# Moving neighbour-row exchange to SyncE transfers and layer-norm scaling to ScalarE in an early-fusion kernel

## The reference, cut to what matters

```
# images: x (8, 1, 256, 256), ten steps of a filter
u = sigmoid(o / 0.5); q = 0
for _ in range(10):
    q = max(q - 0.5 * ((u[y+1] - u[y]) * vf1 + (u[x+1] - u[x]) * vf0), 0)
    Tq = (vf1*q)[y] - (vf1*q)[y-1] + (vf0*q)[x] - (vf0*q)[x-1]
    u = sigmoid((o - Tq) / 0.5)
h_img = (o - Tq) / 0.5                                   # (8, 256, 256)
# text: (8, 128) tokens, width 256, 4 layers, 16 heads, hidden 1024
h = emb[tokens] + positions
for layer in 4: h = norm(h + attention(h) @ Wc) * g1 + e1
                h = norm(h + relu(h @ W1 + b1) @ W2 + b2) * g2 + e2
# fusion: 256 image rows and 128 text rows of each sample
h = concatenate([h_img, h_txt], axis=1)                  # (8, 384, 256)
h = h + window_attention(norm(h)) @ Wo.T + bo            # 8 heads, 2 kv heads, window 64, a sink
y = square(relu(norm(h) @ W_fc.T)) @ W_proj.T
h = h + count_of_spikes(y) / 5                           # five levels of y
```

## Time and profile before

| | |
|---|---|
| median of 3 runs | 1062.35 us (1060.9 to 1063.59) |
| the profiled execution's own time | 1059.45 us |
| its span, first to last instruction | 1057.5 us |
| PE busy | 945.2 us, 89% |
| DVE busy | 900.7 us, 85% |
| ACT busy | 636.8 us, 60% |
| POOL busy | 87.9 us, 8% |
| transfers | 28.67 MB, mean 27 GB/s |
| mean granted TensorE clock | 0.982 of full |

### The profile page before, as it was taken

One profiled execution on the slowest core, in us unless ns is written; L12 is line 12 of the kernel. 1 busy time (PEld: TensorE's weight loads), 2 busy tenths in 40 slices (PEclk: granted clock), 3 DMA queues, 4 the chain that ended last, 5 costly groups with the idle time before them and its releaser, 6 DMA issues.

```text
span 1057.5 us, 18395 instructions
## 1 busy us (share of the span) xinstructions
PE 945.2 (89%) x6972; PEld 714.7 (68%) x6992; DVE 900.7 (85%) x1318; ACT 636.8 (60%) x2105; POOL 87.9 (8%) x149
## 2 busy tenths in 40 slices
PE   3589999889889989989989988789998999999997
PEld 2367777667667767767767766566666766667675
DVE  4999999999999999999999999798699699543542
ACT  1666667766666666666766665446455564745633
POOL 6100010001010010010010001010000001000000
PEclk9799999999999999999999999999999999999999
DMA  7600000110000110000110000000000000100000
GB/s 162 244 1 2 1 30 6 46 61 1 1 31 11 43 39 21 1 31 11 46 55 2 1 21 2 1 11 2 26 1 26 9 18 1 46 25 2 16 1 30
DMA packets 13544, 28.67 MB, mean 27 GB/s; under 512 B 2704, under 2 KB 9232, under 8 KB 12176
## 3 DMA queue, kind: packets, MB, share of 16 engines
q1 hardware_dynamic: 13072, 26.44, 7.5%
q0 software_dynamic: 384, 1.05, 0.6%
HBM read 22.25 MB, written 5.24 MB: 26 GB/s over the span
## 4 chain that ended last, share of the span: by engine, by line
PE 45%; DVE 43%; ACT 7%; issue 4%; DMA 1%; SPq 0%; POOL 0%; POOLq 0%; ACTq 0%; DVEq 0%
PE ps_t L595 8%; PE ps_t L604 7%; PE ps_s L493 4%; DVE neg_max L1544 4%; PE ps_m L808 3%; PE ps_t L797 3%; DVE f L1538 2%; DVE f L1520 2%; DVE f L1516 2%; DVE f L1519 2%; DVE p L1526 2%; DVE f L1511 2%; DVE p L1523 2%; DVE f L1508 2%; DVE f L1533 2%
## 5 line engine op out<-in xcount | busy, mean ns | idle before, releaser
L1010 ACT ACTIVATE prob<-ps_s,neg_max 128x128 f32<-128x128 f32 x512 | 180.1, 379 | 52.2 <-DVE neg_max L1544 52.2
L595 PE MATMUL ps_t<-hT_f,w 128*128 128x256 f32 x512 | 133.0, 404 | 33.1 <-ACT hT_f L1022 17.2
L595 PEld LDWEIGHTS ps_t<-hT_f,w 128*128 128x128 f32 x512 | 95.3, 196 | 58.9 <-ACT hidT L1076 23.9
L1018 ACT ACTIVATE probT<-ps_t 128x512 f32<-128x512 f32 x128 | 77.2, 603 | 83.2 <-PE ps_t L554 52.6
L604 PE MATMUL ps_t<-w,hidT 128*128 128x256 f32 x512 | 125.4, 383 | 0.0
L1010 ACT ACTIVATION_READ_ACCUMULATOR prob<-ps_s,neg_max 128x1 f32 x512 | 112.8, 220 | 0.0
L604 PEld LDWEIGHTS ps_t<-w,hidT 128*128 128x128 f32 x512 | 91.1, 190 | 12.2 <-issue 3.0
L797 PE MATMUL ps_t<-km,w_fc 128*128 128x384 f32 x256 | 94.4, 504 | 1.7 <-ACT km L1183 1.0
L554 PE MATMUL ps_t<-ident,prob 128*128 128x128 f32 x512 | 81.4, 283 | 5.9 <-ACT prob L1010 3.7
L1076 ACT ACTIVATE hidT<-ps_t,b 128x256 f32<-128x256 f32 x128 | 54.8, 491 | 49.8 <-PE ps_t L595 49.8
L554 PEld LDWEIGHTS ps_t<-ident,prob 128*128 128x128 f32 x512 | 63.0, 145 | 28.4 <-issue 11.8
(11 more groups left out here) (172 smaller groups left out, 1879.3 us busy)
## 6 DMA issues: line engine op xcount, KB each, us to landing
w<-in_w SPq DMA_DIRECT2D x8, 1024.0 KB, 4.9
w_attn<-in_w_attn SPq DMA_DIRECT2D x4, 768.0 KB, 4.6
out<-w SPq DMA_DIRECT2D x7, 384.0 KB, 2.4
o_all<-in_o SPq DMA_DIRECT2D x4, 512.0 KB, 10.5
filtered<-f_out SPq DMA_DIRECT2D x4, 512.0 KB, 2.6
x<-filtered SPq DMA_DIRECT2D x8, 256.0 KB, 2.7
vf<-in_vf SPq DMA_DIRECT2D x4, 256.0 KB
w_attn<-in_w_attn SPq DMA_DIRECT2D x4, 256.0 KB, 3.1
```

The costliest lines, as they stand in the source:

```text
L595: last = mm(ps_t[:, 0, D * (m % 2):D * (m % 2) + D], w1[:, c, P * m:P * m + P], hT_f[:, c], start=(c == 0), stop=(c == KC - 1))
L1010: last = A(prob[:, n % 2, hh], ps_s[n % 2][:, hh], ACT.Exp, scale=-1.0, bias=neg_max[:, n % 2, hh:hh + 1], accum_out=den)
L1018: A(probT[:, 4 * half:4 * half + 4].rearrange("p h k -> p (h k)"), ps_t[:, 1], ACT.Copy).then_inc(s["act_pT"], 1)
```

## The change

1. **Neighbour rows.** `u` and `p1` get a fifth row. SP copies it from the neighbouring partition inside SBUF, two transfers of 63 partitions by 1 KB for each of `rows_below` and `rows_above`. The 80 products on PE go, and so do the bank `halo`, the small DVE instructions 1515 and 1537, and the 128x768 forms. Now the whole difference down and the whole divergence down are one pass of 128x1024 each, and wait for a transfer.
2. **The freed bank** (`ps_y`, `row_bank`) takes the attention residual, the turned rows and the odd parts of `ff1`; the even parts stay in `ps_t`, so that `ff1(f, j)` waits for `hidden_out(f, j - 2)`.
3. **Norms on ACT.** POOL also makes `shift = -mean * rstd` (four instructions for two) and ACT scales rows as `rstd * x + shift`. This holds for all norms but the second norm of the last layer and the first `norm_x`. ACT also copies text rows and values; the bias of the values goes into `values_in`.
4. **Orders.** Lists of all engines are written anew, the loads of images and fusion weights are spread over blocks 0 to 5, and on SP the copies are placed between the other transfers.

```
@@ PE
-            def rows_below(it):
-                pe_.wait_ge(s["act_tanh"], it + 1)
-                mm(halo[:, 0], up_shift[:], u[:, 0, 0:IMG], start=True, stop=True).then_inc(s["pe_halo"], 1)
@@ SP
+            def rows_below(it):
+                if it < ITERS * PAIRS:
+                    sp.wait_ge(s["act_tanh"], it + 1)
+                    for at in (0, 64):
+                        sp.dma_start(u[at:at + 63, RPP, 0:IMG], u[at + 1:at + 64, 0, 0:IMG]).then_inc(s["halo_u"], 16)
+            def rows_above(it):
+                sp.wait_ge(s["dve_flux"], it + 1)
+                for at in (0, 64):
+                    sp.dma_start(p1[at + 1:at + 64, 0], p1[at:at + 63, RPP]).then_inc(s["halo_p"], 16)
@@ DVE
...
-                link(stt(fa[:, RPP - 1], halo[:, 0], edge[:], u[:, RPP - 1, 0:IMG], ALU.add, ALU.subtract))
+            def differences_down(it):
+                dve.wait_ge(s["halo_u"], 32 * it + 32)
+                link(tt(fa, u[:, 1:, 0:IMG], u[:, 0:RPP, 0:IMG], ALU.subtract))
                 link(tt(fa, fa, vf[:, 0], ALU.mult))
...
             def divergence(it):
-                dve.wait_ge(s["pe_halo"], 2 * it + 2)
-                link(tt(fa[:, 0], p1[:, 0], halo[:, 1], ALU.subtract))
+                dve.wait_ge(s["dve_flux"], it + 1)
+                dve.wait_ge(s["halo_p"], 32 * it + 32)
+                link(tt(fa, p1[:, 1:], p1[:, 0:RPP], ALU.subtract))
@@ ACT
+            def norm_attn(k):
+                act.wait_ge(s["pool_shift_a"], k + 1)
+                scaled_rows(k, row_bank, rstd_a, shift_a).then_inc(s["act_ln1"], 1)
+            def norm_ffn(k):
+                act.wait_ge(s["pool_shift_f"], k + 1)
+                scaled_rows(k, ps_t[:, 0], rstd, shift).then_inc(s["h_ready"], 1)
@@ PE, ff1
-                else:
-                    pe_.wait_ge(s["act_ff1"], 4 * k + j)
+                elif j >= 2:
+                    pe_.wait_ge(s["act_ff1"], 4 * k + j - 1)
...
             def block_step(a, f, it, its):                        # on ACT
                 exps(a, 0, 0)
-                exps(a, 0, 1)
+                values_out(a)
+                norm_attn(f)
                 probs_out(a, 0, 0)
                 ffn_in(f)
+                exps(a, 0, 1)
...
+                rden_out(a, 0)
                 rden_out(a, 1)
-                filter_out(it + 1)
+                if its > 1:
+                    filter_out(it + 1)
                 if a + 1 < BLOCKS:
-                    keys_out(a + 1, 0)
                     queries_out(a + 1)
                 else:
                     queries_biased(0)
+                if f < BLOCKS - PAIRS:
+                    norm_ffn(f)
```

More of the change, by code:

```diff
@@ L336, in _ @@
             for n in range(B):
+                it = TEXT_ITERS + sum(FUSE_ITERS[:n])
+                for i in range(FUSE_ITERS[n]):
+                    rows_above(it + i)
+                    rows_below(it + i + 1)
+                    pair_done(it + i)
                 if n + 2 < B:
-                    if n + 2 == B - 2:
-                        store_pair(PAIRS - 1)
-                        sp.wait_ge(s["st_img"], 16 * PAIRS + 16)
+                    sp.wait_ge(s["st_img"], 16 * ((n + 2) // 2) + 32)
                     sp.wait_ge(s["f_y"], n + 1)
@@ L963, in fuse_last @@
                 ff_in(f, 2)
+                ff_out(f, 0, range(0, 1))
                 ff_in(f, 3)
@@ L990, in first_tanh @@
             def first_tanh(pair):
-                A(u[:, :, 0:IMG], o_all[:, pair], ACT.Tanh).then_inc(s["act_tanh"], 1)
+                A(u[:, 0:RPP, 0:IMG], o_all[:, pair], ACT.Tanh).then_inc(s["act_tanh"], 1)
             def filter_out(it):
@@ new lines, in fuse_step, with fuse_late @@
+                z_out(n - 1)
+                queries_biased(n + 1)
+                values_in(n + 1)
+                keys_biased(n + 1)
+                norm_y(n)
+                z_last(n - 1)
+                if its > 1:
+                    filter_out(it + 1)
+                window_values(n + 1)
+            def fuse_late(n):
+                x2_out(n - 1)
+                if n + 1 < B:
+                    copy_text(n + 1)
+                relu_out(n - 1, 0)
+                square(n - 1, 0)
+                relu_out(n - 1, 1)
+                square(n - 1, 1)
+                tile_exps(n, 0, 0)
+                relu_out(n - 1, 2)
+                tile_exps(n, 0, 1)
@@ L1582, in scaled_rows, with norm_ffn_last @@
+                moments(rows_of(ps_t[:, 0]), 2, s["dve_stat_f"])
+            def norm_ffn_last(k):
+                dve.wait_ge(s["dve_stat_f"], k + 1)
+                dve.wait_ge(s["pool_rstd_f"], k + 1)
+                hp, rows = h[:, 2 * (k % PAIRS):2 * (k % PAIRS) + 2], rows_of(ps_t[:, 0])
+                scaled = [tick(stt(hp[:, t], rows[:, t], mv[:, t, 0:1], rows_last[:, 0], ALU.subtract, ALU.mult)) for t in range(2)]
                 for t in range(2):
                     dve.wait_ge(s["chain"], scaled[t])
-                    last = stt(hp[:, t], hp[:, t], rstd_[:, t:t + 1], rows_last[:, 1], ALU.mult, ALU.add)
@@ L1851, in fuse_late @@
                 moments_y(n)
-                norm_y(n)
                 count_spikes(n - 1, 0)
```

778 lines of the change are left out of this document (400 added, 378 removed).

## The result

The changed kernel takes **1108.2 us** (median of 4 runs, 1107.1 to 1109.7) against 1061.6 before (4 runs, 1060.8 to 1063.6): ratio 1.0437, 95% interval 1.0416 to 1.0458. The forecast was 1030.5 us, range 1014 to 1052. It was wrong in sign.

The account below looks back on a forecast made before the run. DVE was taken to bound text, PE close behind, and PE to bound fusion. 1059.45 - 21.0 - 4.2 (text) + 3.7 (start) - 10.2 (fusion) = 1027.7 us profiled, 1030.5 as median; range 1014 to 1052.

Parts of the forecast that it names:

- Part 1: DVE work in a steady text block: falls from 39.15 to 36.83 us without small forms, both norms and a wait.
- Part 2: Next text block's first DVE pass, no longer covered by norm_ffn, waits 0.57 us for Tanh; block 37.40 us, 1.75 less.
- Part 3: Copies of neighbour rows in text blocks: a pair lands after 2.4 us, inside 3.4 us of other DVE work, costing nothing.
- Part 4: PE in a text block: work 34.1 us fits in 37.4, row chain 0.5 us slower, DVE stays bound by 0.8.
- PE and ACT hold the block: Rival for text blocks: they stay near 38.5 to 39 us, gaining 0.4 instead of 1.75; 1050 us, chance 0.15.
- Part 5: Start: differences_down(0) waits for a copy queued behind 2.5 MB, there at about 30 us; +3.7 us (0 to +5.5).
- Part 6: Fusion, bound by PE: halo products -5.4, PE's waits -3.6, fuse_first about 2 us gained, last norm_y +0.8; sum -10.2 us.
- the pair serializes: Rival for the copies: two full landings one after the other, 3.9 us, each wait up to 0.5; 1051 us, chance 0.07.

Follow-up runs that it names:

- e6: The changed kernel with one wait added: DVE stands behind the first norm's moments until POOL's shift_a is there, in text blocks and the first fusion step; 1074.1 us, ratio 1.0112.
- e12: e10 with DVE's second head maximum right behind the moments and the wait for POOL behind that maximum; 1056.2 us, ratio 0.9934 to the kernel before.
- e1: The changed kernel with head_max(a, 1) moved on DVE's list from behind flux_rows to right behind moments_attn; 1088.8 us, ratio 1.0252 to the kernel before.
- e3: The changed kernel with eight unread products of 128x256 on PE between turn_probs(a, 0, 0) and turn_ffn(f); 1078.0 us (one run).
- e8: e7 with eight unread PE products before the turn of the rows and the first pair of copies issued ahead of two 1 MB loads; 1061.0 us, ratio 0.9983.
- e7: e6 with the same DVE wait for POOL behind the moments of the y rows in fusion too; 1067.9 us, ratio 1.0058 to the kernel before.
- e10: e8 with ACT's fusion list reordered: norm_x(n + 1) behind o_out(n), z_last(n - 1) ahead of norm_y(n); 1058.9 us, ratio 0.9974 to the kernel before.

## Why the prediction was wrong, by its own steps

- **Part 1, right.** 36.83 us of DVE work in a block: 36.83 and the waits shown make 40.88 of 40.91, and in e6 38.79 of 38.77.
- **Part 2, right** in mechanism: 0.46 us of wait for Tanh instead of 0.57.
- **Part 3, right that copies cost nothing in a block, mis-sized by a microsecond.** I had a pair there 2.4 us (2.1 to 3.1) after the producer. In e12 `flux_rows` starts at 302.88 and lasts 1.22, and the pass on copied rows starts at 307.71, **3.6 us** after its end. The cover of 3.4 to 3.5 us is about as long, so in the changed kernel hardly a wait shows (3.6 us in 6 places); where e1 and e12 took the maximum out of that cover it showed at once. Issuing a pair takes 1.44 us on SP, 0.72 each, where I had taken 0.43; the other 0.9 us lies in the landing.
- **Part 4, the step that failed.** "Moments, then four POOL instructions instead of two, then ACT instead of DVE, about 0.5 us more." I priced POOL's instructions by rows in which DVE read PSUM beside them, and the change itself put other passes there. The chain took 3.6 us, not 1.4, and PE's wait before the turn 3.60 us. The second half, "PE idles some 2.7 us around `turn_ffn` and `ff1(f, 0)`", costed PE's idle time but not the slower products after it: 2.2 us a block (e3). The row chain, from moments to turn, got 4.81 - 2.21 = 2.6 us longer and not 0.5. PE's work itself was right: 34.03 us in a block of e6 at a granted clock of 1.00, forecast 34.1. "DVE stays the bound with 0.8 us to spare" was then off by 4.4. The rival "PE and ACT hold the block" named the right place, and its sign was seen (DVE waits for PE before the maxima, 54.9 us in 16 places), but it had the wrong mechanism and half the price; it ended at 1050.
- **Part 5, mis-sized**: +7.1 instead of +3.7, outside its bound of 5.5. The first pass on copied rows starts at 33.19 us, after a wait of 7.9, not at 30.3. The small copies queued behind 2.5 MB came last. Issued ahead of the two 1 MB loads (e8) they cost 1.6 us over before.
- **Part 6, wrong in sign**: +17.6 instead of -11.0. The halo products went, but three costs came, by the profiles' stages: the clock on entering from the text stage (5.7 us between e7 and e8, e7's being a slow execution), the y chain held by passes (4.2, e6 to e7), the x chain seen through ACT's order (3.9, e8 to e10). The sum of 13.8 leaves 3.8 us over before, which no run here explains; ACT's longer lists remain the candidate. The forecast gain of 11.0 had no term for any of them.
- **The rival "the pair serializes"**, at 1051: not in the form it had, two full landings one behind the other. In e12 the pair of `p1` is issued from 304.13 on, and two stretches hold its data (last column GB/s), before DVE goes on at 307.71:

```profile
305.35:306.05 0.70, 0.70 (x5) 0.62 (x4) 0.70 (x1) 0.70 (x3) 0.00 (x0) 1.00 0.30 92
306.05:306.85 0.80, 0.80 (x6) 0.70 (x5) 0.45 (x1) 0.80 (x6) 0.00 (x0) 1.00 0.30 86
```

  The second copy's data moves 0.7 us behind the first's, which is the distance of the two issues. Whether copies issued closer together would queue, no run here shows.

The profile of the kernel before held the warning: in its fusion stage the `pow`, on 128x3 there, took 0.85 us in most steps and 1.73 and 1.92 in others (at 689.29 and 800.38). I had not asked why.

## What to carry to other kernels

A short chain on a side engine has the price of its neighbours. When an order moves, look again at what runs *beside* each small instruction on the path, above all GpSimd beside VectorE passes with both inputs in SBUF. Put VectorE work that reads PSUM there, or let it stand for a microsecond; the wait added here was worth 34 us. And an idle stretch of PE can cost more than its length: count the products that follow it at the lower clock, and give PE something to do if the stretch can't be closed.

## What the runs showed of the hardware that was not expected

- A POOL instruction of 128x2 that begins beside a DVE pass of 128x1024 with both inputs in SBUF ends about 0.05 us after it (1.01 to 1.08 us instead of 0.20, in all 16 first norms), and a `pow` about 0.55 us after it (1.55 instead of 0.69). It is not held where the DVE instruction is the head maximum, which reads PSUM. An instruction that begins in the gap between two passes takes 0.19 (`neg_mean_a`), so one instruction in four slipped through. Nor is one held that began before the pass: in the kernel before, the second norm's `pow` started 0.10 us ahead of a pass on SBUF and took its usual time, and so did the pass. One that started 0.01 us behind a pass (800.38, on 128x3) took 1.92 us instead of 0.85.

```profile
370.67 0.70 POOL L404 TENSOR_TENSOR rstd<-var_eps,pow_half 128x2 f32<-128x2 f32 x1
370.77 1.23 DVE L1538 TENSOR_TENSOR f<-f 128x1024 f32<-128x1024 f32 x1
```

- The hold seems to work one way here: the DVE passes beside POOL instructions took their usual 1.19 to 1.25 us.
- After 3.60 us of idle time PE ran 5.9 us at a granted clock of 0.52, close to the lower level. After 2.19 us idle `ff1(f, 0)` was as slow (3.78 us, e1). After 1.4 us idle the clock fell in some blocks of e6 (3.31 us for the eight products, from 347.59) and not in others (1.99 us from 308.82, the block at 1.00).
- A copy inside SBUF of 63 partitions by 1 KB occupies SP for 0.72 us, against 0.43 for a 1 MB load of 128 partitions. A pair of them is usable 3.6 us after the producer's end (e12), longer than the 2.6 us of a small load behind others.
